# GNN attention and MoE feed-forward layer: the adjacency cast while it is loaded, another set-up order, masks made three units ahead instead of four

## The reference

```python
x = x + gnn(layernorm(x), adj, W_seq, a1, a2, W_out, b_out)
x = x + ffn(layernorm(x)[None], gate, ..., up_w, down_w)[0]

def gnn(x, adj, W_seq, a1, a2, W_out, b_out):     # N = 2048, 16 heads of 32
    seq = (x @ W_seq).reshape(N, H, DH)
    score1, score2 = einsum('nhd,d->hn', seq, a1), einsum('nhd,d->hn', seq, a2)
    scores = leaky_relu(score1[:, :, None] + score2[:, None, :], 0.2)
    scores = scores + (1.0 - adj)[None] * -65500.0
    attn = softmax(scores, axis=-1)
    hidden = einsum('hij,jhd->ihd', attn, seq).reshape(N, D_IN)
    return elu(hidden @ W_out + b_out)
```

## Time and profile before

| | us |
|---|---|
| median of 3 runs (1056.38 to 1060.91) | 1058.4 |
| the profiled execution | 1060.79 |
| its span in the profile | 1058.9 |
| set-up, until PE's first attention matmul | 99.8 |
| 32 attention units | 99.8 to 487.9 |
| everything after | 571 |
| PE busy, share of the span | 95% |
| DVE busy, share of the span | 76% |

### The profile page before, as it was taken

The page is one execution under the profiler, slowest core; times in us unless marked ns, Lnnn a source line. Parts: engine busy times, 40 slices in busy tenths (PEclk is TensorE's granted clock), DMA queues, the critical chain, the costliest instruction groups (busy, mean ns, idle before and its releaser), DMA issues.

```text
span 1058.9 us, 27195 instructions
## 1 busy us (share of the span) xinstructions
PE 1006.7 (95%) x11256; PEld 890.0 (84%) x11256; DVE 803.9 (76%) x1197; ACT 666.5 (63%) x990; POOL 251.5 (24%) x271
## 2 busy tenths in 40 slices
PE   5996889999999999999899999999999999989998
PEld 4875889999999999997677888888888877778887
DVE  6776899999999999993699433448775668975554
ACT  2668999999989889933356333344454546655431
POOL 1103124334333443363331000000065000006500
PEclk9996999999999999999899999999999999999999
DMA  8781111111111111623635000020063124453242
GB/s 301 249 313 40 41 62 43 45 61 42 43 52 52 42 43 52 225 67 132 229 116 208 1 1 1 1 80 1 26 207 117 50 80 131 130 158 112 85 134 99
DMA packets 53778, 102.45 MB, mean 97 GB/s; under 512 B 6161, under 2 KB 26257, under 8 KB 53138
## 3 DMA queue, kind: packets, MB, share of 16 engines
q1 hardware_dynamic: 47666, 82.83, 23.6%
q0 software_dynamic: 3072, 8.39, 2.5%
q10 hardware_dynamic: 2928, 9.57, 2.4%
HBM read 74.69 MB, written 26.08 MB: 95 GB/s over the span
## 4 chain that ended last, share of the span: by engine, by line
PE 47%; issue 2%; DVE 2%; DMA 1%; POOL 1%; ACT 0%; SPq 0%; POOLq 0%; DVEq 0%; ACTq 0%
PE bank L1758 16%; PE bank L1291 16%; PE bank L668 3%; PE bank L1835 2%; PE bank L1786 1%; PE bank L1787 1%; PE bank L1789 1%; DMA xs<-sorted_latent_rows 1%; PE bank L1805 1%; PE bank L1779 1%; PE bank L1743 1%; PE bank L1741 1%; PE bank L665 1%; PE bank L1740 1%; DVE acc_rest L1492 0%
## 5 line engine op out<-in xcount | busy, mean ns | idle before, releaser
L730 ACT ACTIVATE arena<-arena 128x1024 fp8e4<-128x1024 f32 x320 | 336.6, 1136 | 2.5 <-ACT arena L722 1.6
L956 PE MATMUL bank<-arena 128*128 128x132 f16 x4096 | 285.6, 222 | 19.0 <-DVE arena L816 7.6
L956 PEld LDWEIGHTS bank<-arena 128*128 128x128 fp8e4 x4096 | 246.6, 98 | 20.8 <-issue 8.6
L1291 PE MATMUL bank<-xt,up_parts 128*128 128x512 f32 x768 | 186.2, 391 | 0.0
L1758 PE MATMUL bank<-down_parts,h_parts 128*128 128x512 f32 x768 | 184.5, 389 | 0.1
L960 PE MATMUL bank<-arena 128*128 128x66 f16 x4096 | 173.5, 196 | 0.0
L794 DVE TENSOR_SCALAR arena<-arena 128x1024 uint8<-128x1024 f32 x192 | 167.8, 940 | 2.7 <-DMA arena<-s_rows 2.7
L1758 PEld LDWEIGHTS bank<-down_parts,h_parts 128*128 128x128 f32 x768 | 143.9, 188 | 30.5 <-issue 0.5
L1291 PEld LDWEIGHTS bank<-xt,up_parts 128*128 128x128 f32 x768 | 142.3, 188 | 28.6 <-ACT relu_sb L1240 0.2
L960 PEld LDWEIGHTS bank<-arena 128*128 128x128 fp8e4 x4096 | 154.9, 98 | 0.0
L1265 DVE TENSOR_TENSOR relu_sb<-relu_sb 128x512 f32<-128x512 f32 x64 | 44.4, 693 | 118.0 <-ACT relu_sb L1240 110.9
(11 more groups left out here) (231 smaller groups left out, 1403.9 us busy)
## 6 DMA issues: line engine op xcount, KB each, us to landing
hid<-in_adjT SPq DMA_DIRECT2D x32, 512.0 KB, 5.8
arena<-s_rows SPq DMA_DIRECT2D x30, 512.0 KB, 3.7
sorted_latent_rows<-zeros SPq DMA_DIRECT2D x1, 4992.0 KB, 18.5
xs<-sorted_latent_rows SPq DMA_DIRECT2D x39, 128.0 KB, 2.1
sorted_expert_rows<-expert_y SPq DMA_DIRECT2D x39, 128.0 KB, 1.7
arena<-in_x SPq DMA_DIRECT2D x4, 1024.0 KB, 10.8
xr<-in_x SPq DMA_DIRECT2D x16, 256.0 KB, 2.8
up_sb<-in_upT ACTq DMA_DIRECT2D x1, 4096.0 KB, 14.0
```

The source lines that it names most:

```text
L730: last = nc.scalar.activation(m8[:, k, j, :], s1b[:, k % 2, :], ACT.Sigmoid, bias=bias_now[:, k % 2, j:j + 1], scale=STEEP, saturate=False)
L956: last = nc.tensor.matmul(o, m8[:, k, j, i * P:(i + 1) * P], vs[:, b, j, :], start=(j == 0), stop=(j == T - 1))
L1291: last = nc.tensor.matmul(bank[6 + s % 2][:, :], sa[:, s % 2, a, k, :], xt[c][:, b, k, :], start=(i == 0), stop=(i == len(mm) - 1))
```

## The change

Set-up:
- The adjacency isn't loaded as float32 any more. POOL issues eight DMAs (four for each half of the columns, 2 MB of float32 each) whose destination is the fp8 array, so the cast happens in the transfer. All 32 casts on DVE and ACT go, and the ring of buffers. The first four are issued when the first four tiles of x are there, the other four after the fourth `root`. Entries are now +1 in place of -1, and the flags of empty rows change with them.
- The weight comes in four pieces, each with its own mean (DVE) and subtraction (ACT), transposed and split piece by piece. The constants come through ACT's queue, x in five pieces.
- Scores are made earlier between the projections, `degrees(1)` comes before the last three of these, and the first s1 rows are stored and read back by SP in a small transfer of their own. `copy_v(7)` now stands on ACT behind the exponentials.
- Head 0's values are made in two parts (tiles 0 to 11 by POOL, 12 to 15 by DVE), and unit 0 starts with the first part for three of its tiles.

Attention: DVE's and ACT's steps for unit u make the masks of u+3, and `mask_acts` is for u+2. The buffers of the first four units are numbered 0, 2, 1, 3.

```diff
@@ set-up: loads
-            for q in range(HALVES):
-                if q >= AB:
-                    sp.wait_ge(cast_by_act if (q - AB) % 2 else cast_by_dve, (q - AB) // 2 + 1)
-                sp.dma_start(adj_in[:, q % AB, :], adjT[(q % T) * P:(q % T + 1) * P, (q // T) * IC:(q // T + 1) * IC]
-                             ).then_inc(adj_loaded[q % AB], 16)
+            for c in range(KD):
+                sp.dma_start(wt_sb[:, c, :], w_seqT[c * P:(c + 1) * P, :]).then_inc(wt_loaded[c], 16)
...
+            sp.wait_ge(st_copied, 6)
+            sp.dma_start(s1_dram[0:2, 0:IC], s1_rows[0:2, 0:IC]).then_inc(s1_stored, 16)
...
@@ set-up: POOL
+            def load_adjacency(half):
+                cols = slice(half * IC, (half + 1) * IC)
+                for g in range(AG):
+                    pool.dma_start(adj8[:, 4 * g:4 * g + 4, cols],
+                                   adjT[512 * g:512 * g + 512, cols].rearrange("(j p) i -> p j i", p=P)
+                                   ).then_inc(adj_loaded[half], 16)
+
+            pool.wait_ge(x_loaded[1], 16)
+            load_adjacency(0)
             for g in range(4):
                 root(g)
+            load_adjacency(1)
             largest(0, slice(H, H + 1))
             pool.wait_ge(var_ready, 5)
...
@@ set-up: ACT
+            copy_rows(0, 1)
             copy_v(6)
...
+            copy_rows(2, 3)
             act.wait_ge(expin_ready, 1)
             nc.scalar.activation(coef.rearrange("p h t c -> p t h c")[:, :, :, 0], zval, ACT.Exp)
             nc.scalar.activation(coef.rearrange("p h t c -> p t h c")[:, :, :, 1], zneg, ACT.Exp)
             nc.scalar.activation(bval, nval, ACT.Exp).then_inc(act_step, 1)
+            copy_v(7)
...
@@ set-up: PE
             project(7)
-            scores_to_rows()
             degrees(0)
-            project(8, 9, 10, 11, 12, 13, 14, 15)
+            project(8, 9, 10, 11, 12)
             degrees(1)
+            project(13, 14, 15)
...
@@ attention: DVE
-                        if k or not first:
-                            dve.wait_ge(unit_in_psum, 4 * p + k + 1)
-                            collect(p, k)
-                        if not last:
-                            if k >= 2:
-                                low_values(p + 1, k % 2)
-                            compare(p + 1, k)
-                            mask_own(p + 1, k)
-
-                        if k == 0:
-                            mask_acts(p, 3)
-                        elif not last:
-                            mask_acts(p + 1, k - 1)
+                        dve.wait_ge(unit_in_psum, 4 * p + k + 1)
+                        collect(p, k)
+                        if not last and k >= 2:
+                            low_values(p + 1, k % 2)
+                        if not last or k == 0:
+                            compare(p + (k + 3) // 4, (k + 3) % 4)
+                            mask_own(p + (k + 3) // 4, (k + 3) % 4)
+                        if not last or k < 2:
+                            mask_acts(p + (k + 2) // 4, (k + 2) % 4)
@@ attention: DVE, before the loop
                 dve.sem_inc(sums_ready, 2)
                 dve.wait_ge(seq_in_psum, 8)
                 compare(0, 0)
-                cast(26)
                 mask_own(0, 0)
-                cast(28, 30)
                 any_neighbour(1)
-                low_values(0, 0)
-                mask_acts(0, 0)
-                dve.wait_ge(seq_in_psum, T)
                 compare(0, 1)
                 mask_own(0, 1)
+                mask_acts(0, 0)
+                low_first(0, slice(0, T_A))
+                apply_empty_rows((2,))
+                products_first(slice(T_A, T))
+                low_first(1, slice(T_A, T))
+                apply_empty_rows((3,))
+                compare(0, 2)
+                mask_own(0, 2)
                 low_values(0, 1)
                 mask_acts(0, 1)
...
@@ attention: POOL
-                        pool.wait_ge(m_ready, 4 * p + k + 3)
+                        pool.wait_ge(m_ready, 4 * p + k + 2)
```

More of the change, by code:

```diff
@@ L48 @@
 MB = 4
-AB = 5
-HALVES = 2 * T
+AG = 4
 UNITS = H * NIC
@@ L256, in setup_act @@
-            cast(11)
+            copy_scores(3)
             copy_v(5)
-            copy_scores(3)
-            cast(13, 15)
+            copy_rows(0, 1)
             copy_v(6)
-            cast(17)
-            copy_v(7)
-            for c in range(4):
-                act.wait_ge(st_in_psum, 5 + c)
-                nc.scalar.copy(s1_rows[:, c * 512:(c + 1) * 512], ROW_BANK[c][0:H, :]).then_inc(st_copied, 1)
-            act.wait_ge(st_copied, 8)
-            act.dma_start(s1_dram[:, :], s1_rows).then_inc(s1_stored, 16)
@@ L268, in setup_act @@
-            cast(19)
-            copy_v(8)
-            cast(21)
-            act.wait_ge(s1_stored, 16)
-            for k in range(2):
-                act.dma_start(s1b[:, k, :], s1_dram[k:k + 1, 0:IC].to_broadcast([P, IC])).then_inc(s1_staged[k], 16)
-            copy_v(9)
+            copy_rows(2, 3)
             act.wait_ge(expin_ready, 1)
@@ L554, in setup_pe @@
             pe.wait_ge(consts_loaded, 48)
-            pe.wait_ge(w_centred, 1)
-            transpose_w()
+            for c in range(KD):
+                transpose_w(c)
             transpose(0, 1)
-            pe.wait_ge(w_ready, 1)
+            pe.wait_ge(w_ready, KD)
             project(0)
@@ L715, in _ @@
             def _(act):
-                copy_v, cast = setup_act(act)
+                copy_v = setup_act(act)
                 def compare(p, k):
@@ L788, in _ @@
             def _(dve):
-                cast, any_neighbour, apply_empty_rows = setup_dve(dve)
+                any_neighbour, apply_empty_rows = setup_dve(dve)
                 def compare(p, k):
@@ L831, in split_low, with body @@
                     nc.vector.tensor_scalar(ones_r[0:1, :], ident2[0:1, :], 0.0, 1.0, ALU.mult, ALU.add).then_inc(wo_low, 1)
-                def body(p, last=False, first=False):
+                def body(p, last=False):
                     for k in range(4):
@@ L950, in _, with products @@
                         pe.wait_ge(m_ready, 4 * p + k + 1)
-                        for i in range(IT):
+                        def products(i, tokens):
                             g, slot = GROUP_OF[i]
@@ L963, in _ @@
                                         start=False, stop=False, skip_group_check=True)
+                            return last
+                        ahead = [t0 for t0, n in GROUPS] if p == 0 and k == 0 else []
+                        for i in ahead:
+                            if i == ahead[-1]:
+                                pe.wait_ge(v_copied, T - 1)
+                            products(i, range(T_A))
+                        if ahead:
+                            pe.wait_ge(lo_ready, 2)
+                        for i in ahead:
+                            products(i, range(T_A, T))
+                        for i in range(IT):
+                            if i not in ahead:
+                                last = products(i, range(T))
                         last.then_inc(unit_in_psum, 1)
```

338 lines of the change are left out of this document (173 added, 165 removed).

## The result

The changed kernel takes 1071.68 us (median of 4 runs, 1069.59 to 1073.51), the kernel before 1059.66 beside it (4 runs). The ratio is 1.0114, with a 95% interval of 1.0091 to 1.0138: **1.1% slower**. The forecast was 1064, the range 1048 to 1083, and "slower by over 0.5%" had the largest chance, 0.50. Sign and range held. The size did not: 12.0 us between the medians, where the prediction had 5.6.

The account below looks back on a forecast made before the run. The prediction took DVE's mask steps to set the attention's pace. A start 3.2 us earlier and 9.0 lost in the loop gave +5.8, 1066.6 for the profiled execution, 1064 us for the median, range 1048 to 1083.

Parts of the forecast that it names:

- Casts and SP at 0: Set-up: dropping the casts counts only through earlier first masks; SP's small store and read back has spare time, booked 0.
- Weight and constants at 0: Set-up: first projection can start some 4 us earlier, worth nothing because the next term holds PE back later; booked 0.
- POOL's chain: Set-up: four DMA issues add 4.4 us ahead of 24.1 us that nothing shortens; `exponents` starts at 65.6, not 60.3.
- Units 0 and 1: Attention start: DVE's work from `exponents` on sums to 44.7 us without real idle time, so unit 1 starts at 110.4.
- Units 2 to 9: Early attention: unit 4 at 152, 1.7 us lost there to a lower clock, unit 9 at 214.2, ahead by 3.2 us.
- Three units ahead: Attention loop: DVE and PE wait for each other, 48.75 us a pair for 46.96; 9.0 us lost over five pairs.
- The sum: Unit 31's start: -3.2 from the start plus 9.0 from the loop gives +5.8 us.
- The signs named in advance: Right if PE waits twice a pair, 48.7 us a pair, `exponents` about 65, reconfigurations 7 to 8 us, unit 5 near 165.
- The pace holds: Rival, loop: POOL's values no longer meet the compares in long steps, a pair costs 47.2 us, total 1054.6; chance 0.20.
- Issues are dear: Rival, set-up: POOL's DMA issues cost 4.4 us each, total 1077, or 1087 if the first four slip too; chance 0.17.
- The cast transfer is slow: Rival, set-up: at half rate the adjacency takes 85 us and `any_neighbour(1)` waits until 94, total 1078; chance 0.10.
- Set-up gains more than I book: Rival, set-up: POOL's reconfigurations overlap other work or transfers, up to 8 of 24 us go, total 1056; chance 0.08.

Follow-up runs that it names:

- Experiment 6: The changed kernel with the weight's transposes waiting for all four centred pieces, ACT centring all four before its first copy: 1074.18 us, ratio 1.0148.
- experiment 1: The changed kernel with the four DMA issues of the adjacency's second half moved behind the last partition_all_reduce: 1071.65 us, ratio 1.0115.
- experiment 7: The changed kernel with set-up reordered, including both adjacency halves issued first and the weight's root behind both reductions: 1056.46 us, ratio 0.997.
- experiment 2: The changed kernel with all eight DMA issues of the adjacency ahead of the first root: 1063.07 us, ratio 1.0033.
- experiment 3: The changed kernel with the weight's root behind the second reduction, so both reductions share one reconfiguration: 1065.76 us, ratio 1.0062.
- experiment 4: The changed kernel with masks four units ahead, x's parts moved: 1069.34 us with leftover ACT waits, 1061.12 us in a second build without them.
- experiment 5: The kernel before with masks three units ahead and nothing else of the change: 1076.17 us, ratio 1.0151.
- experiment 10: experiment 8 with the four DMA issues of the adjacency's second half back behind the roots: 1049.25 us, ratio 0.9916.
- experiment 8: experiment 7 with masks four units ahead, as in the second build of experiment 4: 1044.69 us, ratio 0.9848.

## Why the prediction came out as it did

*Casts and SP at 0.* Nothing in the traces speaks against either; no run changes one of them alone.

*Weight and constants at 0.* Wrong as an argument. Experiment 6 prices what the four pieces give in this order at about 2.5 us. The step that failed was "worth nothing by itself if the next term holds PE back later": what the weight moves is not PE's end but the last root, from which the next term starts. The prediction had fixed that start from the tiles' order alone, and by luck nearly hit it: it had the last root end at 37.1, and it ended at 37.51. So this mistake costs the sum only 0.4 us.

*POOL's chain.* The mechanism was right, the size wrong. Of the booked 4.4 us the issues took 3.06. "24.1 that nothing shortens" holds 22.70 of reconfigurations and, for the rest, the instructions between them; the 22.70 failed both ways. The three came to 28.05 in the changed kernel, 20.8 with both halves issued first and 18.6 with idle DMA engines. The exponents began at 69.97 instead of the forecast 65.6: 0.4 from the last root and 5.3 from the reconfigurations, less 1.3 from the cheaper issues. I had read three durations within 0.8 us of each other as a constant, and they held only for that kernel's traffic and order. The Trainium skill (GPSIMD Engine Reference, Instruction dispatch) gives about 6 us for a load of code with no instruction of its own in the profile; experiment 1's 5.80 to 6.87 agree, the 9.59 and 12.15 don't.

*Units 0 and 1.* 44.7 us were given for the way from the exponents to unit 1 (the items add up to 44.85); it took 47.05. DVE's compare takes 4.93 there, not 4.1, and two of the second half's ORs 1.77 and 1.92, not 1.22 (both beside POOL's products).

*Units 2 to 9.* Forecast 165.4 for unit 5 and 214.2 for unit 9, measured 168.87 and 217.66: 3.5 late at both, and the "ahead by 3.2" is gone. Two errors nearly made up for each other here. Unit 4 began 5.2 us late, 4.4 of it from the exponents and 0.8 from the stretch between. But the 1.7 us booked for unit 4 at a lower clock did not come: unit 5 starts 11.52 us after it, as unit 17 does after unit 16. That was luck. Unit 4 in the changed kernel and in experiment 7 (start:end, us, engines' busy, granted clock, DMA share, GB/s):

```profile
157.35:168.87 11.52, 11.52 (x257) 11.52 (x258) 11.18 (x12) 10.54 (x11) 2.74 (x3) 1.00 0.13 48
```

```profile
140.54:154.50 13.96, 13.96 (x256) 13.96 (x257) 11.18 (x12) 10.54 (x11) 2.74 (x3) 0.81 0.24 78
```

PE had waited 3.55 us ahead of the first and 3.46 ahead of the second. Unit 4 took 11.5 us in experiment 2, 12.95 in experiment 1, 12.73 in experiment 3 and 14.15 in experiment 6, always behind a wait of 2.9 to 3.7 us. Whether the clock falls after it can't be told from the length of the wait, so at this place up to 2.6 us stay open in any forecast.

*Three units ahead.* 48.75 us a pair forecast, 48.76 measured, and waits of 0.59 and 1.78 for "0.3 to 0.5 and 1.3". From unit 9 to 29 the loss is 10.0, not 9.0: the last four units before 29 lose 2.8 instead of 1.8. The term's mechanism and size were right, and experiments 4 and 5 show that it needs nothing else of the change.

*The sum.* +5.8 forecast for unit 31, +10.45 measured. The difference: 4.4 from the late exponents, 0.8 on to unit 4, less 1.7 for the clock loss that did not come, 1.0 more at the loop's end and 0.2 in the two units behind it. So the term with the wrong size is the reconfigurations, 5.3 us too short, and without the luck at unit 4 the miss would have been larger. The total stayed in the range, though not within the forecast's own 1057 to 1071. The signs named in advance say the same: the pair and its waits came as written; "`exponents` at about 65", "reconfigurations still 7 to 8 us" and "unit 5 near 165" did not. The medians stand 12.0 apart, the profiled executions 8.8.

*The rivals.* "The pace holds" fell on the pair. "Issues are dear" fell: 0.81 us each for the first four, beside a DVE that is busy 7.34 of the 10 us from 8 to 18, and 0.77 for the others; the lock of the Trainium skill (SBUF — State Buffer, Who interferes with whom) isn't seen in them. That the reconfigurations behind the issues would be longer (9.59 and 12.15 us, against 6.64 and 8.19 in experiment 2) was in no rival. "The cast transfer is slow" fell: the 102 to 104 GB/s from 40 to 60 us, counted in bytes of fp8, are over 400 of float32, and DVE didn't wait for the second half. Its wait came in experiment 1, not because the transfer was slow but because the issue came 19 us later. "Set-up gains more than I book" described what the same change gives in another order: experiment 7 against the changed kernel is 15.2 us.

## What to carry to other kernels

When two engines are each busy over 95% of a loop and one makes work for the other in steps of unequal length, the distance between them pays for averaging: a unit less cost 10.6 us here, and hardly anything was saved by it, since another engine held the start. A GpSimd reconfiguration is not a constant: group the instructions that share one, put what only a later step needs behind them, and keep DMA issues away from the front of them (worth 4.6 us by the medians in experiment 10). Before moving a transfer out of a chain's way, work out when it will land; experiment 1 won 13 us and lost them on the same data.

## What the runs showed that I had not expected

Reconfigurations of GpSimd, by what stood ahead of them: 5.80 to 6.87 us with idle DMA engines (experiment 1), 6.01 to 8.19 with a transfer issued long before, in flight or just over (experiments 2 and 8), 9.1 to 10.1 right behind four DMA issues, and 10.4 to 12.15 for the next one in the same kernels, which began at 50.5 to 53.7 us. In experiment 3, where that second one began at 57 us, it took 7.57. Why this is so stays open: with equal DMA shares the amount of traffic alone doesn't set it, and no run held the issues without their transfer. One pattern is in the traces: those of 10.4 to 12.15 us all ended 0.7 to 2.7 us after the last packet of the second half (61.01 us in the changed kernel, where the root starts at 62.65). But in experiment 2 one of 8.19 us was over 4 us before that packet, and those right behind the issues were over 10 us before it, so a wait for the end of the transfer is not shown. A wait that an edit leaves behind in an engine's program, with no work attached to it, cost 8 us (experiment 4).
